# Score matmuls for the exponential issued as two of 256 columns instead of one of 512

## The reference, cut to what matters

```
x = x + tanh(g_xattn) * attention(layernorm(x), ctx, ctx)     # x (32,128,512), ctx (32,128,128), all float32
x = x + tanh(g_ffn)   * moe(layernorm(x))                      # 8 experts, hidden 256, top 2

# attention: 32 query heads of 16, 8 key/value heads of 16 (k = v = ctx), 4 query heads share one
scores  = einsum('bkgsd,bktd->bkgst', qh, kh) / 4
weights = softmax(scores, axis=-1)
out     = einsum('bkgst,bktd->bkgsd', weights, vh)
```

## Time and profile before

| | us |
|---|---|
| median of 3 runs | 835.18 (834.79 to 835.53) |
| profiled execution | 836.46 |
| its span | 834.7 |
| PE busy | 647.8 |
| DVE busy | 564.9 |
| ACT busy | 358.3 |

### The profile page before, as it was taken

How to read it: one execution, slowest core, us unless ns; L and a number is a source line. 1 busy time by engine, 2 the same in 40 slices (tenths; PEclk the granted TensorE clock), 3 DMA queues, 4 the chain that set the end, 5 groups by cost and what they waited for, 6 DMA issues and landing times.

```text
span 834.7 us, 18064 instructions
## 1 busy us (share of the span) xinstructions
PE 647.8 (78%) x5064; PEld 437.1 (52%) x5065; DVE 564.9 (68%) x1506; ACT 358.3 (43%) x664; POOL 287.9 (34%) x455
## 2 busy tenths in 40 slices
PE   3789999989999998999993599999999999600000
PEld 2444554444444444545432489989899999400000
DVE  3567787787777777877736377777777777454444
ACT  2366666666666666666641133333333333100000
POOL 4123544544545545445325000000000000178885
PEclk9999999999999999999976699999999999955555
DMA  5233343443443444443213545444444446599986
GB/s 164 79 95 93 133 146 118 134 124 129 130 123 138 132 119 142 132 116 104 102 63 114 214 150 155 153 143 151 146 151 150 152 153 191 177 353 351 302 251 214
DMA packets 64767, 129.08 MB, mean 155 GB/s; under 512 B 8400, under 2 KB 12496, under 8 KB 64464
## 3 DMA queue, kind: packets, MB, share of 16 engines
q1 hardware_dynamic: 54032, 94.92, 36.0%
q0 software_dynamic: 10240, 33.56, 11.8%
q10 hardware_dynamic: 448, 0.02, 0.0%
HBM read 74.20 MB, written 54.26 MB: 154 GB/s over the span
## 4 chain that ended last, share of the span: by engine, by line
PE 69%; DVE 11%; POOL 9%; DMA 4%; issue 4%; ACT 1%; POOLq 1%; SPq 0%; DVEq 0%
PE s_ps L889 12%; DVE nmax L629 9%; PE bank_a L868 8%; PE st_ps L912 7%; POOL y L473 6%; PE st_ps L1021 4%; PE st_ps L1020 4%; PE st_ps L1022 4%; PE bank_c L929 4%; PE s_ps L1004 4%; PE st_ps L920 3%; PE bank_b L877 2%; DMA y<-expert_out,g_idx 2%; PE bank_c L1033 2%; PE bank_b L1033 2%
## 5 line engine op out<-in xcount | busy, mean ns | idle before, releaser
L629 DVE TENSOR_REDUCE nmax<-s_ps 128x8 f32<-128x1024 f32 x128 | 156.3, 1221 | 94.4 <-PE s_ps L889 90.7
L889 PE MATMUL s_ps<-k_t,q_t 32*128 32x256 f32 x1024 | 153.5, 418 | 39.0 <-DVE nmax L629 36.9
L505 ACT ACTIVATE probs<-st_ps 128x1024 f32<-128x1024 f32 x128 | 131.1, 1024 | 116.0 <-PE st_ps L920 113.8
L912 PE MATMUL st_ps<-q_t,k_t 32*128 32x512 f32 x512 | 147.9, 653 | 0.9 <-ACT probs L505 0.7
L889 PEld LDWEIGHTS s_ps<-k_t,q_t 32*128 32x128 f32 x1024 | 91.3, 192 | 89.9 <-DVE nmax L629 47.8
L473 POOL DMA_INDIRECT y<-expert_out,rows_all x16 | 15.8, 990 | 275.1 <-SPq L356 270.5
L1020 PE MATMUL st_ps<-w_hi,zh 128*128 x284 | 86.6, 305 | 0.0
L1021 PE MATMUL st_ps<-w_lo,zh 128*128 x284 | 80.8, 284 | 0.0
L1022 PE MATMUL st_ps<-w_hi,zl 128*128 x284 | 80.8, 284 | 0.0
L444 POOL DMA_INDIRECT slots<-z,slot_i x64 | 64.6, 1009 | 16.7 <-issue 16.1
L868 PE MATMUL bank_a<-probs,v_aug 128*32 128x512 f32 x512 | 69.4, 613 | 0.0
(11 more groups left out here) (151 smaller groups left out, 1378.5 us busy)
## 6 DMA issues: line engine op xcount, KB each, us to landing
z_s<-slots SPq DMA_DIRECT2D x71, 256.0 KB, 2.7
expert_out<-y_sb SPq DMA_DIRECT2D x71, 256.0 KB, 2.0
x_in<-in_x SPq DMA_DIRECT2D x32, 256.0 KB, 2.6
wst<-in_w SPq DMA_DIRECT2D x32, 256.0 KB, 2.6
x_res<-in_x SPq DMA_DIRECT2D x32, 256.0 KB
x_scratch<-x_res SPq DMA_DIRECT2D x32, 256.0 KB, 2.0
r_late<-x_scratch SPq DMA_DIRECT2D x24, 256.0 KB
out<-r_late SPq DMA_DIRECT2D x24, 256.0 KB
```

The costliest lines, as they stand in the source:

```text
L505: a.activation(out, st_ps[:, :].rearrange("t (k n) -> t k n", k=2), ACT.Exp, scale=HD ** -0.5).then_inc(exp_done[half], 1)
L629: v.tensor_reduce(out, s_ps[:, :].rearrange("s (r g c t) -> s r g c t", r=2, g=2, c=2), X_AXIS, ALU.max, negate=True).then_inc(max_done, 1)
L889: last = t_.matmul(s_ps[:, HALF * rr + 2 * P * gg:HALF * rr + 2 * P * (gg + 1)], q_t[r2][row:row + ROWS32, P * g_:P * (g_ + 1)], k_t[r2][r ...
L912: t_.matmul(st_ps[:, HALF * rr:HALF * (rr + 1)], k_t[r][row:row + ROWS32, P * i:P * (i + 1)], q_t[r][row:row + ROWS32, :], start=True, sto ...
```

## The change

The pair of 512-column float32 matmuls at L912 becomes two pairs of 256 columns (`raw(0)` and `raw(1)`, L898 in the changed file). The first pair stands where the old pair stood, the second behind `part(1)`. The columns of the first pair are the first half of each bank, and only they carry `start=True`. No wait and no semaphore is moved; the bf16 pair still closes the block.

```
+                    def raw(gg):
+                        for rr in range(2):
+                            row, c0 = ROWS32 * (2 * over + rr), 2 * P * gg
+                            t_.matmul(st_ps[:, HALF * rr + c0:HALF * rr + c0 + 2 * P],
+                                      k_t[r][row:row + ROWS32, P * i:P * (i + 1)],
+                                      q_t[r][row:row + ROWS32, c0:c0 + 2 * P], start=(gg == 0), stop=False,
+                                      tile_position=(row, 0))
...
-                        for rr in range(2):
-                            row = ROWS32 * (2 * over + rr)
-                            t_.matmul(st_ps[:, HALF * rr:HALF * (rr + 1)],
-                                      k_t[r][row:row + ROWS32, P * i:P * (i + 1)],
-                                      q_t[r][row:row + ROWS32, :], start=True, stop=False, tile_position=(row, 0))
+                        raw(0)
                     if valid(b2):
                         part(1).then_inc(s_done, 1)
+                    if valid(b):
+                        raw(1)
```

## The result

| | before | changed |
|---|---|---|
| median | 835.36 us (834.79 to 836.34, 4 runs) | 850.10 us (844.96 to 860.22, 4 runs) |
| ratio of the runs | | 1.0155, 95% interval 1.0081 to 1.0228 |
| profiled execution | 836.46 | 860.22 |
| its span | 834.7 | 858.5 |

On this chip the changed kernel is slower, by 0.8 to 2.3%; the prediction was 835.5 us with a range to 838.8, so it was wrong. Later sets of runs show that the size of the effect is not a property of the two kernels alone.

A forecast was written before the change was run, and what follows sets the result against it. PE and DVE's maxima were taken to alternate in phase 1; 64 block ends on the chain, each 5 ns later, add 0.3 us to the 835.18 median, giving 835.5 us, range 833.5 to 838.8.

The forecast's parts named there:

- What bounds the kernel: Phase 1: PE and DVE's maxima take turns; ends of blocks 0 and 2 and `s_done` of blocks 1 and 3 count.
- Passes on the four row tiles: Inside a block: C and D's bf16 pass starts 5 ns later, A and B unmoved, extra weight loads hidden; 0.3 us.
- The rival by which C and D can't be fed in turn: New second pair on C and D loads weights late, 0.1 us per block, 6.4 us, 841.6; chance 0.15 in all.
- a cost of 25 ns per pass: Skill page's 60-cycle matmul overhead read as a cost of every pass: 3.2 us, sum 838.4; trace showed 2 ns.
- 0 us for `s_done`: Blocks 1 and 3: shorter passes on C and D bring A and B nothing, so `s_done` gains 0 us.
- I can see no gain below zero: A and B have no pause that could be taken out, so no time is saved.
- The phase against the scatter moves: Rival: more or fewer block 3 exponentials fall behind POOL's scatter; 830.6 to 842.4 us; chance 0.12 slower, 0.10 faster.
- the sign that I leaned to: In the phase rival, a later end of block 3 spoke a little for the slower side.
- I priced a late exponential at 0.49 us: Block 0 waiting for block 3's exponential takes 1.78 us to the next work against 1.29 undisturbed: 0.49 each.
- at most 14 more: Some 14 other steady-stretch exponentials of block 3 could fall behind the scatter, besides the 10 already late.
- The top of this case, 842.4 us: Phase rival's slow extreme, if all of some 14 other exponentials fell behind the scatter.
- 10 ns of phase: Change moves block 3's end by about 0.01 us against POOL; a hundredth seemed to tell late exponentials from undelayed.

The follow-up runs named there:

- e2_after_pow: Changed kernel with a 0.57 us power operation on POOL ahead of the two scatters, delaying them; 827.28 us, ratio 0.9997 to the kernel before.
- e2_before_pow: Kernel before with the same power operation on POOL ahead of its two scatters; 826.63 us, ratio 0.9997 to the kernel before.
- e2_adjacent: Changed kernel with both 256-column pairs on C and D ahead of the second pair on A and B; 824.91 us, ratio 0.9990.
- e1_new3: Kernel before with block 3 alone in the new split form; 856.96 us, ratio 1.0265 to the kernel before.
- e1_old3: Changed kernel with block 3 alone in the old form, blocks 0 to 2 new; 833.42 us, ratio 0.9963 to the kernel before.
- e5_done_late: Changed kernel with the maxima released by the last new matmul on C and D; 847.13 us, ratio 1.0142 to the kernel before.
- e1_before_late: Kernel before with POOL's two scatters moved behind the last two small operations of the step; 854.71 us, ratio 1.0226.

## Why the prediction was wrong

**What bounds the kernel:** right. The chain goes by PE and the maxima, until an exponential is late.

**Passes on the four row tiles:** right to the nanosecond rows: 5 ns more per block, weight loads hidden, A and B unmoved. The rival by which C and D can't be fed in turn did not occur (its 0.1 us took the first loads to be through when the second ones start; in the trace of before the second ones start 109 ns behind the first, which last 181); nor did a cost of 25 ns per pass. In a normal block 1 or 3 the next work came 1292 to 1295 ns after the start, against 1287 to 1290, and in block 2 1390 against 1385.

**"0 us for `s_done`", and "I can see no gain below zero":** wrong, by a small gain. The maxima start 42 ns earlier in blocks 1 and 3. I had looked at when A's and B's passes start, and not at when their completion is reported. Where nothing is held it shows: block 3s in e2_after_pow end 12.24 us apart (161.7 to 382.1 us in 18 steps), in e2_before_pow 12.31 (159.6 to 381.2), 70 ns less for 2 x 42 - 2 x 6 = 72. Over phase 1 that is some 2 us, which no median here could tell. I had set aside order on account of the starts alone. The starts do leave the program order; the completions keep to it as far as `s_done` shows them: 1222 ns before, 1180 after, 1226 in e2_adjacent.

**"The phase against the scatter moves":** this is the step that failed, in its size and in its chance. The place was right (the exponential of block 3 beside the second scatter), and so was the sign that I leaned to. I priced a late exponential at 0.49 us, from one held for 0.85, and let at most 14 more fall behind. The 0.49 was too little even for the kernel before: it counts from the start of block 0, which often starts late as well, because the maxima of block 3 are held too. From one block 3 to the next, the steps of before with a held exponential took 13.02 to 13.17 us against 12.34, so 0.7 to 0.8 each. And the delay itself could grow, which I had no term for: in the changed kernel and e1_new3 19 or 20 of 29 were held for 0.6 us or more, half of them for 1.65, where block 0 grows by some 1.27 us and the step by 1.5 to 1.65, and behind a few of them the clock falls. The top of this case, 842.4 us, lay outside my range, and the measured 850 above that. I gave it 0.12 on the slower side, because the three runs of before lay within 0.74 us; but that only says that the kernel before repeats itself, not that its neighbours are near it.

**The reason I gave for it, 10 ns of phase:** not borne out, and the trace of before spoke against it. I compared when the two exponentials of the earlier trace rows started with when the second scatter did. Their input is the bf16 pair:

```profile
172.84 0.38 PE L920 MATMUL st_ps<-nm_t,pick 32*128 32x512 bf16 x2
...
211.31 0.38 PE L920 MATMUL st_ps<-nm_t,pick 32*128 32x512 bf16 x2
```

It ended at 173.22 and 211.69, both times 0.19 us ahead of the second scatter (173.41 and 211.88). So a hundredth of a microsecond did not tell the late one from the other, and the one I took for undelayed was held too, by 0.14. In e1_old3 the second scatter starts 182 to 190 ns after the end of block 3, as in the changed kernel (179 to 188), and 9 are held, as in the kernel before (mostly 190 to 194, 10 held). What matters is the form of block 3 itself. Neither the early release (in e5_done_late as many are held, 19, though only 5 for over 1.5 us) nor the split as such in other blocks (e1_old3) is the cause.

**What stays open.** Where block 3 ends between the two scatters, the records of `st_done` fall near three times after its end (the last one or two steps aside): 0.10 to 0.23, 0.83 to 0.98 and 1.61 to 1.69 us. In the old form `st_done` comes with the first or the second. In the new form (after and e1_new3) it comes with the third in all 21 steps where `s_done` had been held to the first, and with the second in the others, but for the first and the last such step. It looks as if increments leave at turns some 0.75 us apart while the scatters run, and the new block misses one more turn. That reading is argued from the records, not tested: why such turns exist, why they appear in the first runs and in two sets, with before at 835, and not in three others at 825 to 827, and which of the new form's properties (5 ns, more instructions in flight) misses the turn, no run here settles. e2_adjacent would have told the last apart, but it only ran where nothing was held.

## What to carry to other kernels

A profile that shows one wait with two outcomes, 0.04 and 0.9 us, from inputs that look alike, is a warning: any edit that touches the instruction before it may flip the rest, and the price of the whole population belongs in the range, not a few of them. Run the unchanged kernel on more than one chip before pricing tens of nanoseconds: here the same pair of kernels stood at a ratio of 1.0155 in one set and 1.0008 in another. And look at what completion waits for in program order, not only at when passes start: a matmul on another row tile that stood ahead in the order and ended a little later delayed an increment by 42 to 46 ns.

## What the runs showed of the hardware

- Matmul passes on different row tiles start out of program order but seem to report completion in it. The second pass on D started 553 ns into a block and the first pass of B's second matmul, behind it in the order, at 542. The maxima, which B's last pass releases, start 1222 ns into a block when the last pass on D stands ahead of it in the order (before), 1226 with 256-column passes in that order (e2_adjacent), and 1180 when it stands behind (after), though A's and B's passes lie at the same times.
- Beside two indirect DMAs on GpSimd, an increment of TensorE was recorded up to 1.69 us after the end of the matmul that makes it (e1_new3), against 0.016 elsewhere. The second scatter started 0.18 us behind that end. With the first scatter 3.2 us behind it (e1_before_late) none was late, on the same chip.
- In three of five sets no such delay occurred with the same instructions at the same distances, and the kernel before took 825 to 827 us instead of 835.
- A VectorE operation of 512 columns (L654) took 1093 ns in the mean instead of 538 where GpSimd's 512-column operations ran beside it: in e1_before_late 1.04 to 1.14 us in each of 24 steps with 0.7 to 0.85 us of overlap, and 0.54 us in the six without any.
- Behind one of the eleven exponentials held for 1.6 us TensorE's granted clock fell (0.89 in the mean over 15 us, between its two levels), and the step took 1.5 us more than the ten others.
